# A gated recurrence on one core: the scan step's first tanh gets a signal of its own, and the products' first operand is made in two halves

## The reference

```
def step(h, xt):
    m = concatenate([xt, h]) @ weight + bias      # weight 256 x 256
    c = tanh(m[:, 128:])                          # candidate
    g = sigmoid(m[:, :128] + 1.0)                 # gate
    h_new = g * h + (1.0 - g) * c
    return h_new, h_new
x = x + scan(step, cond, x)
x = x + second_block(x, cond)
```

## Time and profile before

| | us |
|---|---|
| median of 3 runs | 517.21 |
| lowest and highest | 515.77, 518.44 |
| the profiled execution's own time | 515.98 |
| its span, first to last instruction | 514.2 |
| PE busy | 378.0 |
| DVE busy | 315.1 |
| ACT busy | 219.9 |
| POOL busy | 155.5 |

### The profile page before, as it was taken

The page is one execution under the profiler, slowest core; times in us unless marked ns, Lnnn a source line. Parts: engine busy times, 40 slices in busy tenths (PEclk is TensorE's granted clock), DMA queues, the critical chain, the costliest instruction groups (busy, mean ns, idle before and its releaser), DMA issues.

```text
span 514.2 us, 13976 instructions
## 1 busy us (share of the span) xinstructions
PE 378.0 (74%) x5187; PEld 258.4 (50%) x5187; DVE 315.1 (61%) x1827; ACT 219.9 (43%) x964; POOL 155.5 (30%) x343
## 2 busy tenths in 40 slices
PE   2998896968576867699999998685977778745050
PEld 1646664746455655465666565363443454534040
DVE  6444444767775758765757764457035468698764
ACT  2233223234343243355454555444875757534230
POOL 6000000131820233800232710443003335556632
PEclk9999999999999999999999999985795775565555
DMA  6109200000000000000000000000000000000000
GB/s 168 49 4 197 52 1 1 2 2 3 2 2 2 2 1 2 3 2 3 1 4 1 2 3 2 2 2 1 3 1 1 1 3 1 21 0 24 0 21 20
DMA packets 8010, 7.88 MB, mean 15 GB/s; under 512 B 1203, under 2 KB 6589, under 8 KB 7942
## 3 DMA queue, kind: packets, MB, share of 16 engines
q1 hardware_dynamic: 7846, 6.72, 5.7%
q0 software_dynamic: 96, 0.26, 0.2%
HBM read 5.91 MB, written 1.07 MB: 14 GB/s over the span
## 4 chain that ended last, share of the span: by engine, by line
PE 53%; DVE 21%; ACT 11%; POOL 7%; issue 6%; DMA 1%; SPq 0%; DVEq 0%; POOLq 0%; ACTq 0%
PE zb L700 18%; PE tb L651 5%; PE tb L793 5%; DVE prod_hi L1289 4%; PE firsts L925 4%; ACT state L1048 3%; PE firsts L836 3%; PE zb L679 3%; DVE prod_lo L1295 2%; PE firsts L857 2%; ACT state L1051 2%; PE zb L904 2%; ACT prd L1170 2%; PE zb L685 2%; POOL stat L521 1%
## 5 line engine op out<-in xcount | busy, mean ns | idle before, releaser
L700 PE MATMUL zb<-prod_hi,whh 128*128 128x8 f16 x1920 | 90.8, 171 | 42.1 <-DVE prod_hi L1289 41.2
L700 PEld LDWEIGHTS zb<-prod_hi,whh 128*128 128x128 f16 x1920 | 73.5, 106 | 95.7 <-DVE prod_hi L1289 88.4
L1048 ACT ACTIVATE state<-zb 128x8 f32<-128x8 f32 x240 | 42.4, 177 | 169.0 <-PE zb L700 169.0
L1289 DVE SCALAR_TENSOR_TENSOR prod_hi<-state 128x16 f16<-128x16 f32 x255 | 47.3, 185 | 98.7 <-ACT state L1051 94.5
L700 PE MATMUL zb<-prod_lo,whh 128*128 128x8 f16 x960 | 63.2, 172 | 2.5 <-DVE prod_lo L1295 0.8
L1295 DVE TENSOR_TENSOR prod_lo<-prod,prod_hi 128x16 f16<-128x16 f32 x255 | 50.4, 198 | 8.7
L515 POOL TENSOR_TENSOR stat<-mv 128x4 f32<-128x4 f32 x8 | 1.6, 201 | 164.8 <-DVE mv L1376 158.8
L1170 ACT ACTIVATE prd<-zb 128x640 f32<-128x640 f32 x64 | 42.1, 707 | 16.6 <-PE zb L904 16.2
L700 PEld LDWEIGHTS zb<-prod_lo,whh 128*128 128x128 f16 x960 | 44.1, 106 | 5.9 <-DVE prod_lo L1295 2.9
L1291 DVE SCALAR_TENSOR_TENSOR prod<-state 128x16 f32<-128x16 f32 x256 | 43.1, 168 | 0.5 <-ACT state L1051 0.5
L1051 ACT ACTIVATE state<-zb 128x16 f32<-128x16 f32 x240 | 42.8, 178 | 0.0
(11 more groups left out here) (291 smaller groups left out, 757.2 us busy)
## 6 DMA issues: line engine op xcount, KB each, us to landing
mod<-ada_rows SPq DMA_DIRECT2D x4, 768.0 KB, 12.2
resid<-in_x_dram SPq DMA_DIRECT2D x6, 128.0 KB, 3.5
out_dram<-state SPq DMA_DIRECT2D x8, 64.0 KB, 2.1
out_dram<-early SPq DMA_DIRECT2D x8, 64.0 KB, 2.1
yy<-in_L_cond_w_ada_dram SPq DMA_DIRECT2D x1, 384.0 KB
early<-in_L_cond_weight_dram SPq DMA_DIRECT2D x2, 128.0 KB
resid<-in_x_dram POOLq DMA_DIRECT2D x2, 128.0 KB, 3.4
w<-in_L_cond_w_f_dram SPq DMA_DIRECT2D x1, 256.0 KB
```

The costliest lines, as they stand in the source:

```text
L700: i = pe.matmul(z_bank(t, k)[:, NB * (t % CH):NB * (t % CH) + NB], whh[:, half, p, k, :], src[:, NB * p:NB * p + NB], start=False, stop=Fa ...
L1048: act.activation(r[:, 24:32], z_bank(t, 1)[:, k:k + NB], ACT.Tanh, scale=-1.0 / ZS)
L1289: dve.scalar_tensor_tensor(prod_hi[:, :], r[:, 16:32], 1.0, r[:, 0:16], ALU.add, ALU.mult).then_inc(hi_ready, 1)
```

## The change

DVE makes `prod_hi` in two instructions of 8 columns. The first, the state's half, waits for the gate's tanh, which is now the first that ACT computes and has its own semaphore `gate_t`; the second, the candidate's half, waits for `cand_t`, the signal of the second tanh. For this the first tanh writes the tanh of the gate (`r[:, 16:24]`), and the second writes candidate and negated gate, both with a scale of -1/ZS, with the candidate's weights and bias negated to match. `step_in` is now counted by DVE's state alone. PE waits for both halves (`hi_ready`, then `hc_ready`) before its eight matmuls; their order is the same. `prod`, `prod_lo` and the state are computed as before. The two waits on `step_in` elsewhere are rewritten for the new counts.

```diff
-        hi_ready, lo_ready = sem("hi_ready"), sem("lo_ready")
+        hi_ready, hc_ready, lo_ready = sem("hi_ready"), sem("hc_ready"), sem("lo_ready")
...
+        gate_t, cand_t = sem("gate_t"), sem("cand_t")
...
-            def z_part(src, half, k, t):
-                for p in range(2):
-                    i = pe.matmul(z_bank(t, k)[:, NB * (t % CH):NB * (t % CH) + NB],
-                                  whh[:, half, p, k, :], src[:, NB * p:NB * p + NB],
-                                  start=False, stop=False, skip_group_check=True)
-                return i
+            def z_part(src, p, half, k, t):
+                return pe.matmul(z_bank(t, k)[:, NB * (t % CH):NB * (t % CH) + NB],
+                                 whh[:, half, p, k, :], src[:, NB * p:NB * p + NB],
+                                 start=False, stop=False, skip_group_check=True)
...
             def step(t):
                 pe.wait_ge(hi_ready, t + 1)
+                if t:
+                    pe.wait_ge(hc_ready, t)
                 for k in (1, 0):
                     for half in range(2):
-                        z_part(prod_hi, half, k, t)
+                        for p in range(2):
+                            z_part(prod_hi, p, half, k, t)
                 pe.wait_ge(lo_ready, t + 1)
-                z_part(prod_lo, 0, 1, t).then_inc(gate_z, 1)
-                z_part(prod_lo, 0, 0, t).then_inc(cand_z, 1)
+                for k, z in ((1, gate_z), (0, cand_z)):
+                    z_part(prod_lo, 0, 0, k, t)
+                    z_part(prod_lo, 1, 0, k, t).then_inc(z, 1)
...
-                        pe.wait_ge(step_in, 2 * STEPS)
+                        pe.wait_ge(cand_t, STEPS)
...
                 act.wait_ge(gate_z, t + 1)
-                act.activation(r[:, 24:32], z_bank(t, 1)[:, k:k + NB], ACT.Tanh, scale=-1.0 / ZS)
+                act.activation(r[:, 16:24], z_bank(t, 1)[:, k:k + NB], ACT.Tanh, scale=1.0 / ZS)\
+                    .then_inc(gate_t, 1)
                 act.wait_ge(cand_z, t + 1)
                 z = firsts[:, :, k:k + NB] if t < FIRST else zb[:, t // CH % 2, :, k:k + NB]
-                act.activation(r[:, 8:24].rearrange("p (a b) -> p a b", a=2), z, ACT.Tanh,
-                               scale=1.0 / ZS).then_inc(step_in, 1)
+                act.activation(view(r[:, 8:9], [16, 2], [1, NB]), z, ACT.Tanh, scale=-1.0 / ZS)\
+                    .then_inc(cand_t, 1)
...
-                    act.wait_ge(step_in, 2 * CH * (c + 1) + (1 if c < NC - 1 else 0))
+                    act.wait_ge(step_in, CH * (c + 1))
...
-                s = ZS * (1.0, 0.5)[k]
+                s = ZS * (-1.0, 0.5)[k]
...
-                dve.wait_ge(step_in, 2 * t + 1)
+                if t:
+                    dve.wait_ge(step_in, t)
+                dve.wait_ge(gate_t, t + 1)
                 if t < STEPS - 1:
-                    dve.scalar_tensor_tensor(prod_hi[:, :], r[:, 16:32], 1.0, r[:, 0:16], ALU.add,
+                    dve.scalar_tensor_tensor(prod_hi[:, 0:NB], r[:, 16:24], 1.0, r[:, 0:8], ALU.add,
                                              ALU.mult).then_inc(hi_ready, 1)
+                dve.wait_ge(cand_t, t + 1)
+                if t < STEPS - 1:
+                    dve.scalar_tensor_tensor(prod_hi[:, NB:2 * NB], r[:, 24:32], 1.0, r[:, 8:16], ALU.add,
+                                             ALU.mult).then_inc(hc_ready, 1)
                 dve.scalar_tensor_tensor(prod[:, :], r[:, 16:32], 1.0, r[:, 0:16], ALU.add,
                                          ALU.mult).then_inc(products, 1)
```

## The result

The changed kernel takes 531.6 us in the median of 4 runs (530.6 to 532.1) against 516.8 of the kernel before: a ratio of 1.029, with a 95% interval of 1.027 to 1.031. It is 14.8 us slower. The forecast was slower by 9.9, in a range of 522.5 to 531.8.

What follows compares the result with a forecast made beforehand. The scan's recurrence was taken as the bound: a 1.06 us step closing over prod_hi's start, prod and prod_lo. Costs of 8.9, 0.7, 0.3 and 0 sum to 9.9; 517.2 + 9.9 = 527.1 us, range 522.5 to 531.8.

Steps and rivals of the forecast that it cites:

- The gate half at 0.28: On DVE, prod_hi's gate half starts 0.28 us after the gate tanh's start, 0.10 behind its end, through a late second wait.
- The two spacings of 0.08 each: On DVE, candidate half 0.08 us behind the gate half, prod 0.08 behind that: prod 0.06 later than before.
- 148 clean steps, 8.9 us: Scan steps with or without DVE side work: each pays 0.06 us, 148 x 0.06 = 8.9 us.
- 12 steps with DVE late, 0.7: Scan steps where other work makes DVE late: one more instruction in front of prod, 12 x 0.06 = 0.7 us.
- 13 with two waits before, 0.3: Scan steps already paying 0.07 for a late second wait: prod 0.02 us later, 13 x 0.02 = 0.3 us.
- 82 steps at 0: Scan steps with PE late, or prod late for another reason: the 0.06 us vanishes, so they pay 0.
- a spacing of 0.09: Upper bound for DVE's start-to-start spacing, from a 16-column instruction: 0.09 us a step, 531.9 us in all.
- PE's wait at 0.11, hidden with 0.02 to 0.03 to spare: PE's late second wait before prod_hi's loads costs 0.11 us instead of 0.05, hidden by prod_lo with 0.02 to 0.03 spare.
- The rival that had PE's wait close the step: PE's loads come 0.14 to 0.16 us behind the candidate half: 4.4 us more, 531.5 us. Chance 0.09.
- The rival on the other side: On DVE, gate half starts 0.03 us behind its tanh, prod 0.01 earlier at best: 515.1 us, not slower. Chance 0.08.
- The waits for the finished states at 0: Waits for the finished scan, cand_t instead of both: release PE at most 0.4 us earlier, where other work is in front: 0.

Runs made afterwards that it cites:

- the first experiment: The changed kernel with DVE's wait for gate_t written in front of the wait for step_in: 517.3 us, ratio to the kernel before 1.0019.

## Why the prediction came out as it did

The direction and the mechanism were right: the pairs with exchanged waits and the run with both halves late show each part by itself. The size was short: 9.9 forecast, 14.8 measured (14.9 in the scan of the profiled run). By its terms:

- *The gate half at 0.28.* Measured 0.28, 0.10 behind its tanh. Right, and the row it was taken from, a step with two waits, was the right one of the two ends.
- *The two spacings of 0.08 each.* Measured 0.084 from the gate half to the candidate half and 0.077 to prod, from the unrounded starts. Both are right. But 0.28 and two spacings of 0.08 make 0.44, 0.07 more than the 0.37 of before, and the prediction took 0.43 to 0.44 and wrote 0.06: the rounding, not a spacing, lost 0.007. A clean step pays 0.067.
- *148 clean steps, 8.9 us.* In these the change made 12.0. Plain ones among them pay 0.067; the stalls and most of the stretched instructions lie in them too.
- *12 steps with DVE late, 0.7, and 13 with two waits before, 0.3.* The 13 made 0.4, 0.02 to 0.03 each but for one of 0.11. The 12 made 0.8: nine of them about 0.07, three 0.03 to 0.05.
- *82 steps at 0.* Those with PE late stayed the same within 0.01 in 49 cases; the hiding held. The others, some of them with prod late beside POOL, were not at 0; together the 82 made 1.7.
- *What was no term at all.* Seven stalls, 2.1 us beyond a step's ordinary 0.067, and the stretching beside POOL, 1.9 us beyond what the forecast had for those 47 steps. These two, and the 0.007, are where the sum failed. The time of 531.6 still lies in the range, 0.2 under its upper end, and that is in part luck: the upper end came from a spacing of 0.09 and from PE's wait closing the step, and neither occurred.
- *PE's wait at 0.11, hidden with 0.02 to 0.03 to spare.* Measured 0.11 to 0.12, and hidden: the run with PE's order exchanged moves the loads by 0.06 and not the step. The rival that had PE's wait close the step gave 531.5 us, close to the measured time, but for a reason that did not occur.
- *The rival on the other side*, the gate's signal met at 0.03, is what the first experiment built. It gave 1.054 to 1.060 a step as its working had it (0.01 less at best), but not less time, as the steps that find DVE late pay 0.07 all the same.
- *The waits for the finished states at 0.* Wrong by 0.5 us in the change's favour: I looked at who waits for the end of the scan, not at the copy, which had been waiting for a tanh that it does not read.

The page "VectorE: DVE Perf Modes" of the Trainium skill, section "The DRAIN you can't avoid", has each DVE operation start only when the one before has emptied the pipeline, and a semaphore between two cost nothing extra. The first did not hold for the halves, which start 0.08 apart and last 0.16 to 0.17. The same section adds that a next operation that is not held starts earlier; the prediction left this out, and these rows agree with it. The second did not hold either where DVE waits for its own result: prod_lo starts 0.20 behind prod, where operations without a wait between them start 0.08 to 0.09 apart. The late second wait is another matter, since it is for a signal of another engine.

Another of its pages, "Perfetto Trace Analysis", section "Identifying Dependency Chains", says that an instruction that waits on several engines may get EventSemaphore instructions with the further conditions in front of it. The traces agree, and show which wait that is. Asked for by its line, the wait that is written second appears as an instruction of its own (DVEq is DVE's sequencer; count, then shortest, median and longest ns). First line 1293 of the changed kernel, which is `gate_t`, then line 1293 with DVE's waits exchanged, which is `step_in`, then line 1287 of the kernel before, where `step_in` stands behind an open `settle` as in the earlier trace rows:

```profile
L1293 DVEq EVENT_SEMAPHORE  x254: 21/21/50, 14.9 to 327.7; - x127
```

```profile
L1293 DVEq EVENT_SEMAPHORE  x254: 21/21/412, 14.5 to 312.6; - x127
```

```profile
L1287 DVEq EVENT_SEMAPHORE  x19: 21/21/21, 98.6 to 254.4; - x19
```

The wait written first has no such instruction and stays on the product. In a clean step of the changed kernel the separate wait starts 0.04 behind the end of the gate's tanh and lasts 0.02, and the gate half starts 0.05 behind its end: 0.10 in all, with rounding, against 0.03 where the late wait is on the product itself. With the waits exchanged the separate one is for the state and is through 0.17 before the gate's tanh even starts, so it costs nothing. On PE it is the same: line 707 is a separate wait of 51 ns in front of the loads, and 0.11 becomes 0.05 when the late one is written first. So the 0.07 is the passage through a separate wait instruction that ends last.

Open: what the stalls are. They come with a late wait in second place on DVE (in three kernels; in the run with the product whole at other steps) and all but one at most are gone from DVE when it is written first, whether the steps are short or long. The traces narrow it down. At all six in the changed kernel the separate wait is met on time, and the time is lost behind it: in steps 7, 28 and 159 before the gate half, in step 123 before the candidate half, in steps 49 and 196 before prod. In five of the six (not in step 28) the DMA records have a transfer of 8 KB of the kind "instruction" that starts 1.32 to 1.39 us behind the gate tanh's start. With DVE's waits exchanged the same transfers come in the same five steps, 0.81 to 0.95 behind, and there is no stall; with the product whole and the late wait second the four stalls on DVE again stand beside such transfers, 1.40 to 1.70 behind. So most of the stalls on DVE go with the places where new instructions are loaded, and that they move when the number of instructions changes would fit. Why a late second wait lets such a place cost 0.2 to 0.4 us, and the other order does not, isn't shown. The 1.2 us behind the scan in the profiled run were not looked into either; the part behind the scan varies between 200.4 and 202.9 us over the profiles of this study, with the kernel unchanged there.

## What to carry to other kernels

Where an instruction needs several signals, write the wait for the one that comes last in front of the others: in a loop of 256 dependent steps that alone was worth 14.2 us of 530. Before splitting an operation so that half of it can start early, find what closes the loop (here the fp32 product and prod_lo, not prod_hi), and count what the extra instruction puts in front of it; a head start pays for it at most. And a wait on a counter that two engines share may be waiting for more than it needs.

## What the runs showed of the hardware that was not expected

A late second wait costs 0.07 us on DVE (0.10 instead of 0.03 behind the signal) and 0.06 on PE (0.11 instead of 0.05), and a second wait that is met early costs nothing that shows. The one written second is a separate instruction in front, 21 ns long on DVE and 51 on PE.

The PEclk of the scan can't be taken as it stands. In the profiled run with DVE's waits exchanged it reads 0.50 (1.2 GHz) from 80 us to the end of the scan, where the changed kernel reads 1.00 (2.4 GHz, in the windows above). The window of that run, and the costliest matmuls behind the products, whose line is the same word for word in both runs (line, engine, count, busy, mean ns):

```profile
90.00:300.00 210.00, 161.61 (x2640) 117.59 (x2640) 159.37 (x1086) 85.26 (x459) 68.86 (x159) 0.50 0.01 2
L796 PE MATMUL tb<-wqkv,tw 128*128 128x192 f32 x48 | 23.7, 597 | 0.0
```

The matmuls take 597 ns in both, and the steps of the scan are as long as in the run with both orders exchanged, which reads 1.00. It would be wrong to conclude that the clock changes nothing. One kind of matmul (line 651, 128 x 128 in fp32) occurs in the scan and behind it. In the kernel before it reads, in the scan at a PEclk of 1.00, then behind it in a stretch at 0.50, then in one at 1.00:

```profile
L651 PE MATMUL tb<-identf,tw 128*128 128x128 f32 x24 | 8.0, 436 | 2.5 <-ACT tw L1089 2.5
```

```profile
425.50:451.50 26.00, 22.65 (x198) 13.85 (x197) 18.34 (x104) 16.87 (x64) 13.56 (x27) 0.50 0.05 11
L651 PE MATMUL tb<-identf,state 128*128 128x128 f32 x4 | 1.1, 435 | 0.0
```

```profile
367.10:387.20 20.10, 16.22 (x290) 8.70 (x282) 5.29 (x18) 16.49 (x40) 1.72 (x4) 1.00 0.01 2
L651 PE MATMUL tb<-identf,O 128*128 128x128 f32 x8 | 1.3, 286 | 0.6 <-DVE O L1500 0.6
```

The scan runs at the pace of the 0.50 stretch: 436 ns beside 435, and 286 where the clock was at 2.4 GHz. The starts of neighbours in such a group say the same: 0.21 to 0.25 us apart in the scan, 0.21 to 0.27 at 0.50, 0.11 to 0.17 at 1.00. The trace of the kernel before has its first clock record at 339.6 us, that of the changed kernel at 355.3; the 1.00 before it stands where there is no record. These matmuls lie between 87 and 266 us in the kernel before, and their mean is 436 or 437 ns in the scan of every run here. So TensorE was at 1.2 GHz there in all of them, whatever was printed: the mean of 0.87 given for the kernel before is too high, and the clock does not tell the versions apart in the scan.
